# First MLP of a conditional-MLP and adapter kernel: VectorE's and ScalarE's instruction lists for units 1 to 7 written in another order

## The reference

```
def cond(x, code, W...):                       # x: (32, 64, 512)
    q, k, v = x @ Wq, x @ Wk, x @ Wv
    a = softmax(q k^T / sqrt(512)) v @ Wp + bp
    c = gelu(a @ cW1 + cb1) @ cW2 + cb2 + one_hot(code)     # first MLP: 512 -> 2048 -> 512
    m = gelu([a, c] @ mW1 + mb1) @ mW2 + mb2                # second MLP: 1024 -> 2048 -> 512
    return clip(x + c + m, 0, 1)
def adapter(x, role, ...):                     # per-batch weights, layernorm
    h = gelu(x @ Wdown[role] + bd[role]) @ Wup[role] + bu[role]
    return layernorm(x + h) * gamma[role] + beta[role]
y = adapter(cond(adapter(cond(x, ...), ...), ...), ...)     # two layers
```

## Time and profile before

| | us |
|---|---|
| median of 3 runs | 2026.36 |
| lowest, highest | 2024.31, 2026.97 |
| the profiled execution's own time | 2024.03 |
| its span (first to last instruction) | 2022.3 |
| busy: TensorE, VectorE, ScalarE, GpSimd | 1998.4, 1631.7, 1104.6, 472.6 |

### The profile page before, as it was taken

One profiled execution on the slowest core, in us unless ns is written; L12 is line 12 of the kernel. 1 busy time (PEld: TensorE's weight loads), 2 busy tenths in 40 slices (PEclk: granted clock), 3 DMA queues, 4 the chain that ended last, 5 costly groups with the idle time before them and its releaser, 6 DMA issues.

```text
span 2022.3 us, 28718 instructions
## 1 busy us (share of the span) xinstructions
PE 1998.4 (99%) x9356; PEld 1662.8 (82%) x9356; DVE 1631.7 (81%) x2513; ACT 1104.6 (55%) x2072; POOL 472.6 (23%) x511
## 2 busy tenths in 40 slices
PE   9999999999999999999999999999999999999998
PEld 8887888888887778888888878888888887888887
DVE  7589987888768987888867897888886789778887
ACT  5476654555357754555436764555544676445552
POOL 0033222321103322233011340233210233132321
PEclk9999999999999999999999999999999999999999
DMA  8411021213421112112471112122243011211143
GB/s 294 177 42 53 32 99 63 73 61 113 162 94 38 43 64 94 50 61 74 153 249 42 42 63 89 37 74 73 70 190 116 32 53 42 99 63 49 62 147 95
DMA packets 43537, 178.22 MB, mean 88 GB/s; under 512 B 5752, under 2 KB 9848, under 8 KB 34936
## 3 DMA queue, kind: packets, MB, share of 16 engines
q1 hardware_dynamic: 43248, 176.36, 24.6%
q10 hardware_dynamic: 144, 0.03, 0.0%
HBM read 151.17 MB, written 25.20 MB: 87 GB/s over the span
## 4 chain that ended last, share of the span: by engine, by line
PE 90%; DVE 4%; DMA 2%; issue 1%; ACT 1%; SPq 1%; POOL 1%; DVEq 0%; ACTq 0%
PE psum L831 83%; PE psum L1160 1%; DMA gains<-roles_in 1%; PE psum L1197 1%; PE psum L906 1%; PE psum L928 1%; DVE wsc L1786 1%; DVE pairs_raw L2022 0%; DVE yt L2454 0%; PE psum L1173 0%; DMA fraw<-fuse_in 0%; PE psum L929 0%; PE psum L908 0%; SPq L522 0%; DVE pairs L1786 0%
## 5 line engine op out<-in xcount | busy, mean ns | idle before, releaser
L831 PE MATMUL psum<-cop,wsm 128*128 128x512 f32 x1416 | 354.7, 389 | 0.0
L2038 DVE TENSOR_TENSOR acc<-psum,acc 128x1024 f32<-128x1024 f32 x216 | 263.4, 1220 | 103.2 <-PE psum L831 102.7
L831 PE MATMUL psum<-aop,wsm 128*128 128x512 f32 x1320 | 333.1, 389 | 0.9 <-DVE wsm L1786 0.9
L831 PE MATMUL psum<-aop,wsc 128*128 128x512 f32 x1320 | 319.9, 390 | 5.0 <-DVE wsc L1786 4.8
L831 PEld LDWEIGHTS psum<-cop,wsm 128*128 128x128 f32 x1416 | 265.8, 188 | 55.1
L831 PEld LDWEIGHTS psum<-aop,wsc 128*128 128x128 f32 x1320 | 246.5, 188 | 60.7 <-DVE wsc L1786 8.1
L831 PEld LDWEIGHTS psum<-aop,wsm 128*128 128x128 f32 x1320 | 247.7, 188 | 52.6 <-issue 1.3
L831 PE MATMUL psum<-hs,wd 128*128 128x512 f32 x768 | 181.3, 390 | 0.5
L831 PE MATMUL psum<-pairs,wdc 128*128 128x512 f32 x672 | 177.0, 392 | 1.7 <-DVE acc L2038 1.1
L831 PEld LDWEIGHTS psum<-hs,wd 128*128 128x128 f32 x768 | 143.9, 188 | 32.2 <-DVE acc L2062 2.2
L831 PEld LDWEIGHTS psum<-pairs,wdc 128*128 128x128 f32 x672 | 124.5, 188 | 34.0 <-issue 8.2
(11 more groups left out here) (222 smaller groups left out, 3762.4 us busy)
## 6 DMA issues: line engine op xcount, KB each, us to landing
w1m<-m_in SPq DMA_DIRECT2D x32, 1024.0 KB, 4.9
w1c<-c_in SPq DMA_DIRECT2D x32, 512.0 KB, 3.5
w<-m_in SPq DMA_DIRECT2D x32, 512.0 KB, 3.5
gains<-roles_in SPq DMA_DIRECT2D x30, 512.0 KB, 4.8
fw<-fused SPq DMA_DIRECT2D x6, 2048.0 KB, 10.9
w<-c_in SPq DMA_DIRECT2D x20, 512.0 KB, 4.4
fused<-fw SPq DMA_DIRECT2D x4, 2048.0 KB, 7.6
xmid<-x SPq DMA_DIRECT2D x4, 2048.0 KB, 8.5
```

Source lines behind the costliest of these rows:

```text
L831: mm = nc.tensor.matmul(out, lhs(a), rhs(b), start=(start and n == 0), stop=(stop and n == total - 1), skip_group_check=reopened)
L2038: nc.vector.tensor_tensor(dst, bank, dst, ALU.add).then_inc(acc_done, 1)
```

## The change

Both `first_units` lists get a new order. Each holds the same entries as before, none added or removed, with the same waits in each helper. TensorE's, GpSimd's and SyncE's programs are the same. The diff, cut to the stretches that the prediction speaks of (first ScalarE's list, then VectorE's):

```diff
             def first_units(p, layer):
 
+                copy_u2(p, 1)
+                copy_p5(p, 1)
                 weight_part(p, 1, P4)
-                copy_u2(p, 1)
                 weight_part(p, 1, P3)
                 hidden(p, layer, 1, H00)
-                copy_p5(p, 1)
-                split_part(p, 1, P5)
                 hidden(p, layer, 1, H11)
+                weight_part(p, 2, P2)
                 weight_part(p, 2, P1)
                 hidden(p, layer, 1, H10)
                 weight_part(p, 2, P5)
-                weight_part(p, 2, P2)
                 weight_part(p, 2, P7)
+                weight_part(p, 2, P4)
                 weight_part(p, 2, P6)
                 copy_p1(p, 2)
-                weight_part(p, 2, P4)
...
+                split_part(p, 2, P2)
+                weight_part(p, 4, P4)
+                split_part(p, 1, P7)
                 weight_part(p, 4, P6)
-                weight_part(p, 4, P4)
-                split_part(p, 2, P2)
-                split_part(p, 1, P7)
-                hidden(p, layer, 3, H10)
+                split_part(p, 2, P7)
                 copy_p1(p, 4)
+                copy_down(p, 2)
                 split_sum(p, 2, P4)
-                copy_down(p, 2)
...
                 split_sum(p, 4, P5)
+                split_part(p, 3, P5)
+                copy_p1(p, 5)
+                split_part(p, 4, P5)
+                split_part(p, 3, P3)
+                split_part(p, 4, P3)
                 weight_part(p, 5, P3)
-                split_part(p, 3, P5)
                 hidden(p, layer, 4, H01)
-                split_part(p, 4, P5)
-                copy_p1(p, 5)
...
                 hidden(p, layer, 7, H00)
                 split_part(p, 6, P7)
                 split_part(p, 5, P4)
-                hidden(p, layer, 7, H10)
                 split_part(p, 6, P4)
-                down_part(p, 7)
                 weight_part(p, 8, P6)
                 weight_part(p, 8, P7)
-                hidden(p, layer, 7, H11)
                 weight_part(p, 8, P2)
                 weight_part(p, 8, P4)
+                down_part(p, 7)
                 hidden(p, layer, 7, H01)
+                hidden(p, layer, 7, H10)
+                hidden(p, layer, 7, H11)
...
                 weight_part(p, 2, P1)
+                weight_part(p, 2, P5)
+                make_z12(p, 1)
                 hidden_sum(p, 1, P5)
-                weight_part(p, 2, P5)
+                weight_part(p, 2, P6)
+                weight_part(p, 2, P2)
                 hidden_sum(p, 1, P6)
-                weight_part(p, 2, P2)
-                weight_part(p, 2, P6)
-                make_z12(p, 1)
...
+                low_part(p, 2, P7)
+                hidden(p, 3, H11)
+                low_sum(p, 2, P6)
+                hidden(p, 2, H01)
+                low_sum(p, 2, P4)
+                make_z12(p, 3)
...
                 fast_add(p, 2, P6)
...
+                hidden_sum(p, 3, P4)
+                weight_part(p, 5, P1)
                 low_sum(p, 3, P7)
-                hidden(p, 3, H11)
+                weight_part(p, 5, P2)
+                make_z22(p, 4)
+                low_sum(p, 3, P6)
                 fast_add(p, 2, P2)
-                make_z22(p, 4)
-                hidden_sum(p, 3, P4)
-                low_sum(p, 3, P6)
                 low_sum(p, 3, P4)
-                weight_part(p, 5, P1)
                 fast_add(p, 2, P7)
-                weight_part(p, 5, P2)
                 hidden_sum(p, 4, P5)
+                make_z12(p, 4)
                 hidden_sum(p, 4, P6)
+                hidden_sum(p, 4, P7)
                 weight_part(p, 5, P6)
-                make_z12(p, 4)
-                hidden_sum(p, 4, P7)
-                hidden(p, 4, H11)
                 low_part(p, 3, P5)
-                hidden(p, 3, H00)
-                low_part(p, 4, P5)
+                weight_part(p, 5, P7)
                 low_sum(p, 4, P5)
+                low_part(p, 4, P5)
...
+                make_z12(p, 7)
                 weight_part(p, 8, P6)
                 weight_part(p, 8, P7)
-                make_z12(p, 7)
+                hidden(p, 7, H00)
                 weight_part(p, 8, P2)
                 weight_part(p, 8, P4)
+                down_part(p, 7)
+                hidden(p, 7, H10)
+                hidden(p, 7, H01)
+                fast_add(p, 6, P4)
                 hidden(p, 7, H11)
-                hidden(p, 7, H01)
-                down_part(p, 7)
-                fast_add(p, 6, P4)
```

More of the change, by code:

```diff
@@ L2217, in first_units @@
[L2217 to L2228 removed]
+                low_part(p, 3, P5)
+                weight_part(p, 5, P7)
@@ new lines, in first_units @@
+                low_sum(p, 4, P5)
+                low_part(p, 4, P5)
+                weight_part(p, 5, P4)
+                weight_part(p, 5, P3)
+                hidden(p, 3, H00)
+                low_part(p, 3, P3)
+                hidden_sum(p, 4, P4)
+                fast_add(p, 2, P4)
+                low_part(p, 4, P3)
+                hidden(p, 4, H00)
+                fast_add(p, 4, P5)
+                weight_part(p, 6, P5)
+                low_sum(p, 4, P7)
+                make_z22(p, 5)
@@ L2263, in first_units @@
                 weight_part(p, 7, P5)
+                low_sum(p, 5, P7)
+                make_z22(p, 6)
+                weight_part(p, 7, P1)
                 weight_part(p, 7, P2)
+                fast_add(p, 4, P2)
+                weight_part(p, 7, P6)
+                fast_add(p, 4, P7)
                 low_sum(p, 5, P6)
-                make_z22(p, 6)
-                hidden(p, 5, H00)
-                fast_add(p, 4, P2)
+                hidden_sum(p, 6, P5)
+                make_z12(p, 6)
```

320 lines of the change are left out of this document (147 added, 173 removed).

## The result

The changed kernel takes 2014.18 us (median of 6 runs, 2012.94 to 2015.46); the kernel before, run beside it, 2025.43 (6 runs, 2024.31 to 2026.97; the first three of them have the median of 2026.36 that the prediction started from). The ratio is 0.9944, 95% interval 0.9931 to 0.9957: 11.25 us less, 0.56%. The direction was right, the gain was larger than forecast (11.25 us against 7.7), and the nearest of the recorded cases is "more than forecast" (2015.9 us). The profiled execution took 2013.07 us with a span of 2011.3, against 2024.03 and 2022.3: 11.0 us less.

A forecast was written before the change was run, and what follows sets the result against it. TensorE was taken to carry 90% of the chain of waits, so only its pauses in four stretches could be won: 9.5 less 1.8 charged gives 7.7 us, from 2026.36 to 2018.7 us. The range was 2015.5 to 2025.5 us.

The forecast's parts named there:

- more than forecast: Rival: no new pause and unit 8's load in time, 10.5 us gained, 2015.9 us; chance 0.08.
- The terms that can go: TensorE's pauses at term 2 P6, fast_down 2 P4, term 5 P6 and fast_down 4 P5: 2.46 us a pass, 9.5 taken.
- Term 2 P6: P5's low part some 0.4 us earlier, P6's unstretched (0.48 less): 0.88 against 0.83 lost; pause goes or leaves 0.1.
- The new tight places: Six places where the new order leaves margins of 0.2 to 0.5 us; none overdrawn, but 0.45 a pass charged in all.
- (2): fast_down 2 P5: make_z12 2 waits for term 2 P3's product, low sum three entries later; margin 0.35 us, before 1.0.
- (3): Term 4 P6: split_part 2 P7 waits for fast_down 2 P1 and now stands ahead of copy_p1 4; margin 0.2 us.
- (4): fast_down 2 P6: VectorE's low_part 2 P7 waits about 0.8 us for ScalarE's split, with others queued behind; margin 0.4 us.
- (5): fast_down 4 P5: its low sum was to come 1.4 us earlier, against 0.9 lost; margin 0.5 us.
- (6): Unit 7's down projection: ScalarE does down_part 7 and hidden H01, H10 behind unit 8's weights; margin 0.5 us.
- the collisions did not move onto the tight places: Rival: VectorE's collisions with GpSimd, 0.55 us each, hit tight places; 2.4 us less gain, 2021.1 us; chance 0.20.
- The pauses did come back elsewhere: Rival: six margins each missed by about 0.4, TensorE loses 2.4 us a pass as now, 2026.4 us; chance 0.15.
- Slower: Rival: VectorE falls behind at in-order waits, results 1.1 us late at six places; 7.2 us more, 2033.6 us; chance 0.12.

The follow-up runs named there:

- e6: The changed kernel with copy_p1 4 moved behind copy_down 2 in ScalarE's list: 2017.62 us.
- e10: The changed kernel unaltered, measured once more over 5 rounds: 2014.57 us, ratio 0.9952 against the kernel before.

## Where the prediction was right, and which step failed

- **The terms that can go**: right. 2.46 a pass was the sum; the four places lost 2.37, 2.49, 2.41 and 2.23 us in the four passes, the slower first matmuls included (0.08 to 0.11 a pause), and lose nothing now. 9.5 in all, as taken.
- **The terms that stay**: right. Term 1 P7 has its 0.62 of idle time and unit 7's hand-overs their 0.28 a piece, slower first matmuls included, in both kernels.
- **Term 2 P6**: right in both halves. P5's low part starts at 137.75 instead of 138.29, 0.38 earlier against TensorE (whose own rows stand 0.16 earlier here), and P6's runs 0.42:

```profile
137.75 0.43 DVE L1786 TENSOR_TENSOR wsc<-comb,wsc 128x256 fp32r<-128x256 f32 x1 [0.45 <-ACT wsc L1366]
...
139.49 0.42 DVE L1786 TENSOR_TENSOR wsc<-comb,wsc 128x256 fp32r<-128x256 f32 x1
```

  What I had not counted comes on top: GpSimd's last sum takes 0.73 instead of 1.12, so P6's low part ends 0.53 ahead of TensorE's start. The run with the swap taken back shows that this carries it without the swap, and the swap alone that it isn't enough by itself.
- **The new tight places**: as distances they were counted well, or too small. From the end of the needed operation to TensorE's start, in pass 0: (1) term 2 P1 0.3 counted, 0.42 measured; (2) fast_down 2 P5 0.35 and 0.38; (3) term 4 P6 0.2 and 0.20; (4) fast_down 2 P6 0.4 and 0.43; (5) fast_down 4 P5 0.5 and 1.16. Term 2 P6 and fast_down 2 P4, which I thought would keep 0.1 to 0.2 of a pause, have 0.53 and 0.80. (6) had no pause. But I took the whole distance for a margin, and left out the hand-over of 0.05 to 0.26 that e6 and the old pauses show: (2), (3) and (4) had 0.12, 0.04 and 0.17 to spare.
- **The step that failed is the charge for the new tight places**: "I charge 0.45 a pass in all", 1.8 us, because "each hand count carries some 0.2 of error". The six places cost 0.07 us in the whole profiled run (fast_down 2 P6 in pass 3). At the three tightest, (2) to (4), the counted distance was right to 0.03 us, not 0.2. An error that can fall either way shifts a margin; it costs only where it is larger than the margin. With 0.04 left at (3), an error of 0.2 the wrong way would have been paid in each pass, so that none was paid rests on the counts being that good, and in part on luck.
- **The second term that was off is the load of unit 8**, "I count nothing for it": 1.1 us of the profiled difference. "Starts some 0.6 earlier" was wrong, it starts as far ahead of TensorE as before; the 1.1 comes from a packet of instructions that fell into the load in the first profile of before and not in the first of after. In e10 one fell into it again, and the difference of the profiled spans is 9.5, my own sum before the charge; 11.0 - 1.1 = 9.9 says the same of the first pair.
- **Why the time lies below the range**: from 2026.36 the sum without the charge gives 2016.9, and with the load 2015.8, against 2015.0 measured. The last 0.8 is within what the runs can tell: the two comparisons gave 11.25 and 10.4 us, with intervals of 8.7 to 14.0 and 6.9 to 12.4. How often the load was slow in the runs without a profile isn't known.
- **"By that rule a new order removes no collision, it only chooses who is hit"**: wrong, and my inference. What the Trainium skill states (SBUF — State Buffer, section "SBUF: two separate sides") is about a VectorE operation with two SBUF inputs beside a GpSimd operation that reads SBUF. A new order can put VectorE's operations on PSUM, and its idle time, beside GpSimd's, and this one did: 28 collisions a pass became 13. My rival's count, one in three such operations hit, was too high as well: it was 28 of 160 before. I had read VectorE's 90% busy as work; 10 to 11.5 us a pass of it was waiting for GpSimd, and 5 are left. That shows at (5): ahead of the low sum of fast_down 4 P5 two operations were stretched by 0.55 each before (193.52 in the earlier trace rows is one) and none is now, which is more than the rise from 0.5 to 1.16. At (2) to (4) it made no difference. My condition for failure, busy time "well over 124 us", came out as 119.18 in the same 137:

```profile
122.00:259.00 137.00, 136.23 (x596) 111.11 (x596) 119.18 (x204) 88.21 (x189) 42.69 (x49) 1.00 0.15 51
```

- **The rivals**: the collisions did not move onto the tight places; they became fewer. The pauses did come back elsewhere where only three moves were made, nearly half of them, so that rival holds for those and not for this whole order. "Slower", a backlog of VectorE, did not come up: it is less busy than before.

## What to carry to other kernels

When operations of two engines stretch each other, a busy share hides the waiting: compare the mean duration of each form with its shortest one before you call an engine nearly full. Put the operations that aren't stretched, here those with an input in PSUM, beside the other engine's, and work out the whole order, since moving the three worst entries returned some 40% of the gain. Where margins are counted from one trace, take off the hand-over between the engines first (0.05 to 0.26 us here), then let a positive margin cost nothing, and look for what varies between executions and passes: here a load, and behind it a packet of instructions.

## What the runs showed of the hardware

- A VectorE operation that reads only SBUF and began during a GpSimd sum took longer by what was left of the sum less 0.14 us, at most 0.55 (0.68 to 1.23, 0.41 to 0.96): 238 of 249 such operations in the two traces' stretches, within 0.02. The other eleven, with over 1.0 left, stood in a row of operations without a gap whose first had begun ahead of the sum: they kept their time, and the sum took longer. No operation was stretched that began without a sum beside it.
- Sums that began beside a VectorE operation on SBUF took 0.74 to 1.72 us; those that began beside one that reads PSUM, or with VectorE idle, took 0.73 to 0.76 (183 of 185). All 133 VectorE operations with a PSUM input that began during a sum kept their own time.
- GpSimd's write of a constant, 0.31 us of the same tile, stretched none of VectorE's operations. The Trainium skill (SBUF — State Buffer, section "SBUF: two separate sides") confines the exclusion, for VectorE operations with two SBUF inputs, to a GpSimd operation that reads SBUF; the trace agrees.
- TensorE, waiting, started 0.05 us after a weight's low part, 0.15 after an add or a copy of a PSUM bank, and 0.26 after a hidden sum's low part.
- One load of 1 MB took 5.4 to 5.8 us from its issue to its landing, and 6.6 to 7.05 in the nine of 52 passes in which a 16 KB packet of the instruction queue started 0.4 to 4.6 us after the issue. Issued ahead of a 512 KB load instead of 0.4 us behind it, it took 4.7 to 4.8.
